# Normed rows as two halves of the positions on 64 partitions each, with the bias of their products added by VectorE

## What is computed

```python
x  = layernorm(h)                                     # 1101 x 64, per batch
sx = einsum('bsh,ndh->bnsd', x, hl_w) + hl_b          # 4 heads of 16
q  = einsum('bnsd,neod->bneso', sx, wq)               # 4 experts a head
k  = einsum('bnsd,nod->bnso', sx, wk);  v = einsum('bnsd,nod->bnso', sx, wv)
att = softmax(einsum('bnesd,bntd->bnest', q, k) * d ** 0.5 + causal)
out = where(sx == 0, 0, einsum('bnest,bntd->bnesd', att, v))
gs  = softmax(out_of_all_experts @ gate_w + gate_b);  mixed = sum_e out_e * gs_e
resid = sx[arange(4), arange(4)]                      # batches 0 to 3, one head each
hn = layernorm(mixed + resid); ... two 16 x 16 layers, norm, a gate over heads
h  = h + result
```

## Time and profile before

| | us |
|---|---|
| runs, median of 3 | 1400.64 (1400.48 to 1404.7) |
| profiled execution | 1396.09, its span 1394.4 |
| TensorE busy | 1100.2 (79%) |
| VectorE busy | 792.6 (57%) |
| ScalarE busy | 755.9 (54%) |
| GpSimd busy | 450.2 (32%) |
| chain that ended last | TensorE 43%, issue 11%, ScalarE 8%, VectorE 6%, GpSimd 3% |

### The profile page before, as it was taken

How to read it: one execution, slowest core, us unless ns; L and a number is a source line. 1 busy time by engine, 2 the same in 40 slices (tenths; PEclk the granted TensorE clock), 3 DMA queues, 4 the chain that set the end, 5 groups by cost and what they waited for, 6 DMA issues and landing times.

```text
span 1394.4 us, 39232 instructions
## 1 busy us (share of the span) xinstructions
PE 1100.2 (79%) x15223; PEld 604.6 (43%) x15223; DVE 792.6 (57%) x1493; ACT 755.9 (54%) x906; POOL 450.2 (32%) x616
## 2 busy tenths in 40 slices
PE   4898538898053799899889889789989988989931
PEld 3455338685031346444345444344434434534410
DVE  4827774316755374476467468458557656752453
ACT  0232124452002575868767767767866876789820
POOL 3000040002411322344343542535434435355431
PEclk9998859995555899999999999989989999999975
DMA  8999059920407427107304603611730730550000
GB/s 152 214 184 214 15 119 197 202 57 1 110 13 134 57 66 115 35 15 141 70 14 109 101 2 89 105 29 41 124 59 15 146 63 15 114 87 3 2 17 10
DMA packets 113981, 113.48 MB, mean 81 GB/s; under 512 B 68072, under 2 KB 85240, under 8 KB 113670
## 3 DMA queue, kind: packets, MB, share of 16 engines
q1 hardware_dynamic: 109776, 110.59, 41.4%
q10 hardware_dynamic: 3733, 0.60, 0.3%
q0 software_dynamic: 320, 0.04, 0.0%
HBM read 88.07 MB, written 22.95 MB: 80 GB/s over the span
## 4 chain that ended last, share of the span: by engine, by line
PE 43%; issue 11%; ACT 8%; DVE 6%; POOL 3%; ACTq 0%; DMA 0%; POOLq 0%; DVEq 0%; SPq 0%
PE b_pso L1983 16%; PE b_pss L1947 14%; ACT b_pb L2062 8%; PE b_psm L2009 4%; PE b_pss L1945 3%; POOL b_pb L2100 2%; PE b_psm L2005 2%; PE b_psm L2026 2%; POOL b_stat L2081 1%; DVE b_rq L2188 1%; PE b_psm L1929 1%; DVE b_ks L2186 1%; PE b_psm L2030 1%; DVE b_squares L2187 1%; PE b_psm L2031 1%
## 5 line engine op out<-in xcount | busy, mean ns | idle before, releaser
L2062 ACT ACTIVATE b_pb<-b_pss 128x1024 f32<-128x1024 f32 (+2 forms) x736 | 649.6, 939 | 308.3 <-PE b_pss L1947 235.4
L1983 PE MATMUL b_pso<-b_pb,b_vop 128*32 128x128 f32 (+4 forms) x4800 | 409.3, 414 | 28.0 <-POOL b_pb L2100 27.9
L2100 POOL TENSOR_SCALAR_AFFINE_SELECT b_pb<-b_pb 128x256 f32<-128x256 f32 (+1 forms) x544 | 259.8, 499 | 504.7 <-ACT b_pb L2062 498.1
L1947 PE MATMUL b_pss<-b_qop,b_kop 97*32 97x512 bf16 (+3 forms) x6144 | 361.0, 337 | 62.1 <-issue 42.4
L1947 PEld LDWEIGHTS b_pss<-b_qop,b_kop 97*32 97x32 bf16 x6144 | 143.2, 97 | 284.4 <-ACT b_pb L2062 153.8
L1983 PEld LDWEIGHTS b_pso<-b_pb,b_vop 128*32 128x32 f32 x4800 | 161.2, 113 | 113.3 <-issue 41.8
L2081 POOL TENSOR_TENSOR b_stat<-b_stat,b_mh 128x18 f32<-128x18 f32 x34 | 110.3, 3263 | 30.2 <-DVE b_stat L2355 18.8
L2276 DVE STREAM_TRANSPOSE b_ot<-b_pso 128x512 f32<-128x512 f32 x64 | 45.9, 717 | 126.6 <-PE b_pso L1983 124.2
L920 PE MATMUL psc<-tz,ub 128*64 128x128 f32 x1152 | 81.0, 286 | 15.7 <-ACT tz L961 8.3
L920 PEld LDWEIGHTS psc<-tz,ub 128*64 128x64 f32 x1152 | 73.1, 143 | 23.5 <-ACT tz L961 11.9
L2009 PE MATMUL b_psm<-b_xt,w_all 65*128 65x384 f32 x144 | 63.4, 562 | 19.0 <-DVE b_rq L2188 16.5
(11 more groups left out here) (394 smaller groups left out, 1315.8 us busy)
## 6 DMA issues: line engine op xcount, KB each, us to landing
b_qop<-qk_parts_b SPq DMA_DIRECT2D x192, 144.0 KB
tz<-taps SPq DMA_DIRECT2D x64, 304.0 KB, 9.5
x<-in_x SPq DMA_DIRECT2D x16, 1024.0 KB, 14.3
qk_parts_b<-b_qs SPq DMA_DIRECT2D x16, 864.0 KB, 5.2
b_kop<-qk_parts_b SPq DMA_DIRECT2D x192, 36.0 KB
qk_parts_b<-b_ks SPq DMA_DIRECT2D x8, 432.0 KB, 3.9
n_late<-id_d SPq DMA_DIRECT2D x1, 2400.0 KB, 9.3
h<-z SPq DMA_DIRECT2D x8, 288.0 KB, 2.8
```

Of the source, the lines that this page charges most:

```text
L1947: mm = pe.matmul(pss[VW * g:VW * g + VW, u % 2, b, col:col + w], lhs, qop[:, n, e, q0:q0 + w], start=True, stop=True, skip_group_check=True)
L1983: mm = pe.matmul(acc, vop[0:P if j < NA - 1 else LAST, j, n, :], rhs, start=(j == 0), stop=(q0 == P * j if x < 2 else j == NA - 1), skip_g ...
L2062: nc.scalar.activation(pb[:, SLOT[un], 0:nb, 0:w], pss[:, s % 2, 0:nb, 0:w], ACT.Exp, scale=float(HD) ** 0.5).then_inc(exped, 1)
L2100: ins = pool.affine_select(out=v_, in_=v_, compare_op=ALU.is_ge, fill=0.0, base=0, pattern=pat, channel_multiplier=-1)
```

## The change

`xt` becomes 128 partitions x 576 positions: the channels of positions 0 to 575 on partitions 0 to 63, those of 576 to 1151 on 64 to 127. The row of ones goes, and with it the bias in the products; `wall` stands twice, on both halves of the partitions, without a bias row. `BLOCKS` lists how the 9 tiles fall on the halves, alternating between them; the middle tile is split in two.

- `turn_rows`: tiles of the lower half of the partitions by transposes, those of the upper by products with the identity, 11 instructions for 9. VectorE takes all out in one copy of 576.
- `tok`, `rmat`: a product per tile on one half or the other, into a bank per half; the middle tile in small pieces. VectorE adds the bias (`vb`, the same on all partitions): three additions for the values' one copy, four for the residual's.
- `feat`: six jobs of two products (lower and upper half, bank 0 and 1) of 288 positions in place of nine products of 384 in five jobs. The bias of a feature is `bcol`, a column; VectorE adds it in the first operation (keys: into `rq`, which gives the banks back at once; queries: into the cast, and again in the difference that gives the banks back).
- `knorm` also waits for `parts`, that is for the second key job as a whole, since the squares are read from `sqk`.
- Slots move: turn 21 to 18, tok 24 to 22, the key jobs 28 and 31 to 26 and 30, the query jobs 37, 41, 45 to 37, 41, 44, 48, qnorm 49 to 52, BOUND 51 to 54, CHECK 25 to 23, fc1, fc2, back 53, 56, 60, 63 to 55, 58, 61, 64.
- In `stage_ssm` two copies make `whad` (head weights twice) and `whab` (head bias on 128 columns), and five more products make `vb` and `bcol`; `vb` and `bcol` are copied out behind the convolution loop, into the place of `wbd`.

```diff
@@ -117,8 +117,11 @@
...
-        self.wbd = sb("w_bd", [NH * HD, WV])
-        self.wall = sb("w_all", [D + 1, WV + NH * VC])
+        over = sb("w_bd", [P, WV])
+        self.wbd = over[0:NH * HD]
+        self.vb = over[:, 0:NH * VC + D]
+        self.bcol = over[:, NH * VC + D:NH * VC + D + 3]
+        self.wall = sb("w_all", [P, WV + NH * VC])
@@ -906,7 +911,12 @@
...
-                pe.matmul(psf[0:D + 1, 1, 0:NH * VC], w.wha[:], w.wvx[:].rearrange("p n c -> p (n c)"), start=True, stop=True).then_inc(wv_done, 1)
+                pe.matmul(psf[:, 1, 0:NH * VC], whad[:], w.wvx[:].rearrange("p n c -> p (n c)"), start=True, stop=True)
+                pe.matmul(psf[:, 1, NH * VC:2 * NH * VC], whab[:], w.wvx[:].rearrange("p n c -> p (n c)"), start=True, stop=True)
+                pe.matmul(psf[:, 1, 2 * NH * VC:2 * NH * VC + D], whab[:], w.wbd[:, WC:WV], start=True, stop=True)
+                for g in range(3):
+                    mm = pe.matmul(psf[:, 1, 2 * NH * VC + D + g:2 * NH * VC + D + g + 1], w.wbd[:, g * P:g * P + P], w.wha[:, D:D + 1], start=True, stop=True)
+                mm.then_inc(wv_done, 1)
@@ -1029,6 +1039,8 @@
...
+                ch.done(cp(whad[:].rearrange("p (u d) -> p u d", u=2), bmid(w.wha[:, 0:D], 2)))
+                ch.done(cp(whab[:], bcast(w.wha[:, D], P)))
@@ -1056,15 +1068,18 @@
...
+                v.wait_ge(wt, 2)
+                ch.done(cp(w.vb, psf[:, 1, NH * VC:2 * NH * VC + D]))
+                ch.step(cp(w.bcol, psf[:, 1, 2 * NH * VC + D:2 * NH * VC + D + 3]))
@@ -1703,6 +1718,10 @@
...
+    HALF, PIECE = LP // 2, LP // 4
+    MIDDLE = NA // 2
+    BLOCKS = [(a + 5 * h, h, P * (a + 5 * h) - HALF * h, P, 0) for a in range(MIDDLE) for h in range(2)]
+    BLOCKS += [(MIDDLE, 0, P * MIDDLE, P // 2, 0), (MIDDLE, 1, 0, P // 2, P // 2)]
@@ -1782,20 +1803,19 @@
...
-        PRO = [(21, "turn", 0), (24, "tok", 0), (28, "feat", ((2, 0), (2, 1))), (31, "feat", ((2, 2),)), (34, "knorm", 0), (37, "feat", ((0, 0), (0, 1)))]
-        PRO += [(41, "feat", ((1, 0), (1, 1))), (45, "feat", ((0, 2), (1, 2))), (49, "qnorm", 0)]
-        EPI = [(53, "fc1", 0), (56, "fc2", 0), (60, "back", 0), (63, "back", 1)]
+        PRO = [(18, "turn", 0), (22, "tok", 0), (26, "feat", (2, 0)), (30, "feat", (2, 1)), (34, "knorm", 0), (37, "feat", (0, 0)), (41, "feat", (0, 1))]
+        PRO += [(44, "feat", (1, 0)), (48, "feat", (1, 1)), (52, "qnorm", 0)]
+        EPI = [(55, "fc1", 0), (58, "fc2", 0), (61, "back", 0), (64, "back", 1)]
...
-        CHECK, BOUND = 25, 51
+        CHECK, BOUND = 23, 54
@@ -1924,9 +1944,14 @@
...
-                    pe.matmul(psm[D:P, 0, 0:P], src[:, NA - 1, :], ident[:], start=True, stop=True)
-                    for a in range(NA - 1):
-                        mm = pe.transpose(psm[0:D, a // 4, a % 4 * P:a % 4 * P + P], src[:, a, :], ident[:])
+                    for a, h, c0, n, off in BLOCKS:
+                        for lo in range(c0 // QT * QT, c0 + n, QT):
+                            x0, x1 = max(c0, lo), min(c0 + n, lo + QT)
+                            out_ = psm[D * h:D * h + D, lo // QT, x0 - lo:x1 - lo]
+                            if n == P and not h:
+                                mm = pe.transpose(out_, src[:, a, :], ident[:])
+                            else:
+                                mm = pe.matmul(out_, src[:, a, :], ident[:, off + x0 - c0:off + x1 - c0], start=True, stop=True)
@@ -1995,29 +2020,37 @@
...
                     if kind == "rmat":
...
-                        for a in range(NA):
-                            mm = pe.matmul(psm[:, 0, a * HD:(a + 1) * HD], xt[:, a * P:(a + 1) * P], wall[:, WC + HD * c:WC + HD * c + HD], start=True, stop=True)
+                        for a, h, c0, n, off in BLOCKS:
+                            r = slice(D * h, D * h + D)
+                            mm = pe.matmul(psm[off:off + n, h, a * HD:(a + 1) * HD], xt[r, c0:c0 + n], wall[r, WC + HD * c:WC + HD * c + HD], start=True, stop=True)
                     elif kind == "tok":
...
-                        for z in range(2):
-                            for a in range(4 * z, 4 * z + 5):
-                                lo, hi = max(NH * VC * a, TOK * z), min(NH * VC * (a + 1), TOK * (z + 1))
-                                mm = pe.matmul(psm[:, z, lo - TOK * z:hi - TOK * z], xt[:, a * P:(a + 1) * P], wall[:, WV + lo - NH * VC * a:WV + hi - NH * VC * a], start=True, stop=True)
+                        for a, h, c0, n, off in BLOCKS:
+                            r = slice(D * h, D * h + D)
+                            if n == P:
+                                o = NH * VC * (a % 5)
+                                mm = pe.matmul(psm[:, h, o:o + NH * VC], xt[r, c0:c0 + n], wall[r, WV:], start=True, stop=True)
+                            else:
+                                for z in range(2):
+                                    mm = pe.matmul(psm[off:off + n, z, 4 * NH * VC:TOK], xt[r, c0:c0 + n], wall[r, WV + NH * VC // 2 * z:WV + NH * VC // 2 * (z + 1)], start=True, stop=True)
                     elif kind == "feat":
...
-                        for i, (g, x) in enumerate(c):
-                            mm = pe.matmul(psm[:, i, 0:FB], wall[:, g * P:g * P + P], xt[:, x * FB:(x + 1) * FB], start=True, stop=True)
+                        g, i = c
+                        for h in range(2):
+                            r = slice(D * h, D * h + D)
+                            mm = pe.matmul(psm[:, h, 0:PIECE], wall[r, g * P:g * P + P], xt[r, PIECE * i:PIECE * i + PIECE], start=True, stop=True)
                     elif kind == "knorm":
+                        pe.wait_ge(parts, (p + 1) * 6 + 2)
@@ -2155,12 +2187,20 @@
...
-                        ch.step(cp(xt[0:D, (NA - 1) * P:], psm[D:P, 0, 0:P]))
-                        give(cp(xt[0:D, 0:(NA - 1) * P], psm[0:D].rearrange("p z q -> p (z q)")))
+                        give(cp(xt[:], psm[:].rearrange("p z q -> p (z q)")[:, 0:HALF]))
                     elif kind == "rmat":
-                        give(cp(resid[:, :, HD * c:HD * c + HD], psm[:, 0, 0:NA * HD].rearrange("p (a d) -> p a d", d=HD)))
+                        for a0, a1, h, lo, hi in ((0, MIDDLE, 0, 0, P), (MIDDLE, MIDDLE + 1, 0, 0, D), (MIDDLE, MIDDLE + 1, 1, D, P), (MIDDLE + 1, NA, 1, 0, P)):
+                            last = tt(resid[lo:hi, a0:a1, HD * c:HD * c + HD], psm[lo:hi, h, a0 * HD:a1 * HD].rearrange("p (a d) -> p a d", d=HD), bmid(vb[lo:hi, NH * VC + HD * c:NH * VC + HD * c + HD], a1 - a0), ALU.add)
+                            if a1 < NA:
+                                ch.step(last)
+                        give(last)
                     elif kind == "tok":
-                        give(cp(vnext[:].rearrange("p a n c -> p (a n c)").rearrange("p (z q) -> p z q", z=2), psm[:, :, 0:TOK]))
+                        w_ = NH * VC
+                        flat = vnext[:].rearrange("p a n c -> p (a n c)")
+                        for h in range(2):
+                            ch.done(tt(flat[:, 5 * w_ * h:5 * w_ * h + 4 * w_].rearrange("p (a q) -> p a q", q=w_), psm[:, h, 0:4 * w_].rearrange("p (a q) -> p a q", q=w_), bmid(vb[:, 0:w_], 4), ALU.add))
+                        ch.wait()
+                        give(tt(flat[:, 4 * w_:5 * w_].rearrange("p (z q) -> p z q", z=2), psm[:, :, 4 * w_:TOK], vb[:, 0:w_].rearrange("p (z q) -> p z q", z=2), ALU.add))
@@ -2169,29 +2209,36 @@
...
                     elif kind == "feat":
-                        i = FEATS.index(c)
...
-                        if g == 2:
-                            dst = lambda t_: ks[:, t_, x * FB:(x + z) * FB].rearrange("p (z q) -> p z q", z=z)
-                        elif x == 0:
-                            dst = lambda t_: qs[:, t_, g, 0:2 * FB].rearrange("p (z q) -> p z q", z=2)
-                        else:
-                            dst = lambda t_: qs[:, t_, :, 2 * FB:]
-                        if i == 0:
+                        g, i = c
+                        at_ = FEATS.index(c)
+                        cut = lambda t_: t_.rearrange("p (z h q) -> p z h q", z=2, h=2)[:, :, i]
+                        dst = (lambda t_: cut(ks[:, t_, :])) if g == 2 else (lambda t_: cut(qs[:, t_, g, :]))
+                        if at_ == 0:
...
-                            ch.done(red(nearest[D:P, x:x + z], psm[D:P, 0:z, 0:min(FB, L - x * FB)], AX.X, ALU.min, apply_absolute_value=True))
-                        ch.step(cp(dst(0), psm[0:m, 0:z, 0:FB]))
-                        ch.step(tt(squares[0:m, slot[c[0]]:slot[c[0]] + z, :], dst(0), dst(0), ALU.mult))
-                        give(tt(rq[0:m, 0:z], psm[0:m, 0:z, 0:FB], dst(0), ALU.subtract))
...
-                        ch.step(cp(dst(1), rq[0:m, 0:z]))
-                        tt(dst(2), rq[0:m, 0:z], dst(1), ALU.subtract).then_inc(parts, 1)
...
+                            rest = rq[0:D]
+                            give(ts(rq[:], psm[:, :, 0:PIECE], bcol[:, 2:3], None, ALU.add))
...
```

(15 more changed lines are left out.)

51 lines of the change are left out of this document (26 added, 25 removed).

## The result

The changed kernel takes 1413.2 us in the median (1410.7 to 1414.5, 4 runs), the kernel before 1400.9 (1400.5 to 1404.7, 4 runs): ratio 1.0080, 95% interval [1.0057, 1.0103]. It is slower by 0.8%, where the forecast was 1374 and faster by 1.9%. The profiled execution went from a span of 1394.4 to 1410.8 us.

What follows compares the result with a forecast made beforehand. TensorE was taken to set the pace in the rewritten part, VectorE close behind. Loop passes -19, first attention pass -7, last passes +0.4, pass without attention -4.6 and convolution +4.0 gave -26 us: 1374, range 1358 to 1401.

Steps and rivals of the forecast that it cites:

- the one on the loop's end: End of a loop pass: moving the bound from slot 51 to 54 was to cost nothing.
- the turn: TensorE's transposes and products of x_n in a loop pass: +0.1 us taken, +0.5 if one behind the other.
- the convolution's delay: Before the convolution loop: VectorE's copies +1.8 us and TensorE's products +2.2, together +4.0, handed on whole.
- Overlap of the halves: Loop pass on TensorE: 64-row products of both halves run together, features -3.0 us, values -1.2.
- The rival without overlap: Halves filling all 128 columns don't overlap: a pass +0.4 to +1.1 us, kernel 1412, slower; chance 0.13.
- Waits: Loop pass, TensorE waiting for VectorE: 1.6 us at the features go, 1.6 come at the key norm.
- VectorE: right: Loop pass: VectorE's keys, queries and copies together were to take 2.1 us more.
- the forecast's 7: First pass with attention: -3.2 us as in a loop pass and four residual products at -0.95 each, -7.
- Net of a pass: Loop pass: terms sum to -4.1 us, a fifth taken off for ScalarE, -3.2 a pass, -19 over six.
- a bound (+9): Convolution stage: +9 us if GpSimd's 10 us operation gets ahead of VectorE's first conv copies.
- a rival with 1379 us: GpSimd's 10 us operation falls ahead of the convolution: 1379 us, inside the forecast's range; no chance given.
- ScalarE as the pace: ScalarE sets the pace, so nothing of TensorE's time reaches the end: 1396 us; chance 0.05.

Runs made afterwards that it cites:

- e2: Changed kernel with 64 already satisfied waits added on TensorE's queue ahead of the passes: 1397.1 us, 1.0046 of before.
- e16: e8 run again unchanged on the chip of e13 to e15: 1364.0 us, 0.9773 of before.
- e9: Kernel before with TensorE's loop over passes 1 to 6 written out: 1358.8 us, 0.9727 of before.
- e14: e8 with the five products and two copies moved behind the convolution loop: 1357.6 us, 0.9713 of before.
- e7: Changed kernel with the edits of e1 and e2 together: 1391.1 us, 0.9905 of before.
- e8: Changed kernel with TensorE's loop over passes 1 to 6 written out, other engines keeping theirs: 1366.8 us, 0.9778 of before.
- e10: e8 with a turn that takes two blocks in one transpose: 1357.9 us, 0.9716 of before.
- e11: e8 plus two-block turn, key norm waiting on the squares, and the convolution's five products and two copies behind its loop: 1333.4 us, 0.9537 of before.
- e13: e8 with the turn back in slot 21, the values in slot 24 and the value check in 25: 1369.4 us, 0.9815 of before.
- e15: e11 with the turn in slot 21 and the values in slot 24: 1327.3 us, 0.9457 of before.
- e5: Changed kernel run once more, unchanged: 1417.8 us, 1.0139 of before.
- e1: Changed kernel with whad and whab copied later and the five products with their copy behind the convolution loop: 1404.7 us, 1.0063 of before.
- e6: Kernel before with 176 already satisfied waits on TensorE's queue ahead of the passes: 1396.5 us, 0.9990 of before.
- e12: Kernel before with 216 already satisfied waits on TensorE's queue ahead of the passes: 1401.8 us, 1.0049 of before.

## Why the prediction was wrong, step by step

The step that failed most is the one on the loop's end: the prediction let nothing there cost time and had no term for the loading of TensorE's code (15 us by e2). Two terms failed in size: the turn, at +0.1 us a pass, measured +1.1, and the convolution's delay, at +4.0 us, measured +14.1 at its first product.

The two kernels with TensorE's loop written out give the layout's account in a pass at full clock. Windows of such a pass, of e16 and of e9:

```profile
594.60:698.10 103.50, 95.55 (x1607) 46.36 (x1603) 72.67 (x141) 80.96 (x95) 46.73 (x74) 1.00 0.41 76
```

```profile
591.40:696.40 105.00, 97.59 (x1589) 48.91 (x1585) 70.53 (x132) 81.35 (x95) 47.60 (x74) 1.00 0.41 74
```

Groups of TensorE in these passes, e16:

```profile
L2045 PE MATMUL b_psm<-b_xt,w_all 64*128 64x288 f32 x24 | 4.5, 455 | 0.0
L1958 PE MATMUL b_psm<-w_ident,b_xn 128*64 128x64 f32 (+1 forms) x14 | 1.9, 262 | 0.0
...
L1956 PE MATMUL b_psm<-w_ident,b_xn 128*64 128x128 f32 x4 | 1.2, 292 | 0.0
L2036 PE MATMUL b_psm<-w_all,b_xt 64*128 64x112 f32 x16 | 1.1, 283 | 0.0
...
L2051 PE MATMUL b_psm<-b_sqk,w_blkkb 64*96 64x384 bf16 x2 | 0.5, 326 | 1.7 <-DVE b_ks L2242 1.7
L2039 PE MATMUL b_psm<-w_all,b_xt 64*64 64x56 f32 x8 | 0.4, 228 | 0.0
```

and e9:

```profile
L2013 PE MATMUL b_psm<-b_xt,w_all 65*128 65x384 f32 x18 | 7.1, 515 | 1.1 <-DVE b_rq L2192 1.1
L2009 PE MATMUL b_psm<-w_all,b_xt 65*128 65x112 f32 (+1 forms) x20 | 2.5, 279 | 0.0
...
L1933 PE MATMUL b_psm<-w_ident,b_xn 128*64 128x128 f32 x8 | 1.1, 276 | 0.0
...
L2018 PE MATMUL b_psm<-b_squares,w_blkkb 64*96 64x384 bf16 x2 | 0.5, 326 | 0.5 <-DVE b_rq L2192 0.5
L1931 PE MATMUL b_psm<-w_ident,b_xn 128*64 128x128 f32 x2 | 0.4, 298 | 0.0
```

The turn of these two passes by the windows of `b_xn`, again e16 and e9:

```profile
594.60:698.10 103.50, 2.54 (x18) 1.00 0.41 76
```

```profile
591.40:696.40 105.00, 1.43 (x10) 1.00 0.41 74
```

- **Overlap of the halves: right.** Features 7.1 to 4.5 us, -2.6 (forecast -3.0; a job is 0.76 us, not 0.69), values 2.5 to 1.5, -1.0 (-1.2). The rival without overlap, 1412 us, came near the measured time by a mechanism that isn't there.
- **Waits: right.** 1.6 to 1.7 us (forecast: 1.6 go, 1.6 come). **VectorE: right**, +2.1 us a pass (70.53 to 72.67).
- **The turn, "I take +0.1": mis-sized, +1.1.** 1.4 us became 2.5, beyond the +0.5 of my upper bound. The timelines show why, first before and then changed:

```profile
593.26 0.43 PE L1927 MATMUL b_psm<-w_ident,b_xn 128*64 128x128 f32 x2
593.63 1.06 PE L1929 MATMUL b_psm<-w_ident,b_xn 128*64 128x128 f32 x8
```

```profile
715.37 0.30 PE L1952 MATMUL b_psm<-w_ident,b_xn 128*64 128x128 f32 x1
715.60 0.43 PE L1954 MATMUL b_psm<-w_ident,b_xn 128*64 128x128 f32 x2
715.96 0.30 PE L1952 MATMUL b_psm<-w_ident,b_xn 128*64 128x128 f32 x1
716.19 0.43 PE L1954 MATMUL b_psm<-w_ident,b_xn 128*64 128x128 f32 x2
```

  A transpose and a product for the other column half start 0.23 us apart, and the next transpose 0.36 us later, 0.59 a pair. Before, a product takes 0.37 us to the next start and eight transposes in a row 1.06, 0.13 each: 0.50 for one of each, one behind the other. So the pair, which shares all 128 rows, does not run side by side. I had carried over the overlap of row halves to column halves, for which no row of mine stood, and even my bound without it was too low. It also holds for the four turns of pass 0's residual, which I had left out of that pass's sum: 10.25 us of TensorE (windows of the tile `b_h`) where before has 6.02, while the residual products gave 3.5 (8.7 to 5.2). These 4.2 us and the turn's own 1.1 or more (that pass was not all at full clock) are as much as pass 0, with 1.9 us won, is short of the forecast's 7, though no run separates them. Pass -1, whose turn at 1.2 GHz goes from 2.5 to 4.1, won 3.5 up to the first score and not 4.6. The first score itself came 11.0 us later (453.3), not 0.6 earlier.
- **Net of a pass.** In the two passes above -1.5 us (forecast -3.2); but the three intervals of e9 wholly at full clock take 105.0 to 105.1 us and those of e16 and e14 103.6, 105.1 and 103.4, so it is -1.0 in the mean. In the kernels that keep the loop and have no second stall at the 14th record it is about as much: 557.3 and 557.4 us over five passes in e2 and e7, before 564.4, -1.4 a pass. Written out, nothing is left over all five passes (105.8 in e9, 106.0 in e8, 105.3 in e16): TensorE was at 1.2 GHz for 31 us in e8 and 17 in e16, and 7 in e9. The other written-out profiles of the new layout have 31 (e10), 17 (e11, e13), 27 (e14) and 10 us (e15), all more than the single one of e9. The reason is not shown; e13 speaks against the turn's slot.
- **"The bound's move costs nothing", and nothing else at the loop's end: the step that failed most.** The prediction had no term for code. The changed kernel stands a second time 14 records behind its loop's top, as it would if a 16 KB block of its code ended there: 10.4 us in itself, 15 us by e2. The five intervals were forecast to gain 16 us and lost 8; of these 24 us e2 gives back 15, and the turn's 1.1 or more a pass makes up most of the rest. The trace of before showed the 4.5 us of "issue" at the loop's top, which I had read as given.
- **The convolution stage, "+4.0": right for VectorE's delay, wrong for what follows from it.** VectorE came 4.5 us later, and so just past the start of GpSimd's 10 us operation; the first product came 14.1 us later instead of 4.0. I had this as a bound (+9) and as a rival with 1379 us "inside the range", without comparing the two starts: 196.3 + 4.0 = 200.3 against 200.5 in the trace, a margin of 0.2 us. In other profiles (e2 to e5, e16) one copy slipped in ahead, the first product came at 201.9 to 203.2 and the loop still ended at 304. e1 and e14 took away the delay and the hold together, and the loop's end was back at 292 to 293. The Trainium skill, Advanced Engine Details and Errata, section VectorE Performance Modes, says that a VectorE instruction that uses two ports and a GpSimd instruction block each other. The traces agree, for whab (8.48 us beside GpSimd's copy, where whad takes 0.18 just ahead of it) and for tz.
- **ScalarE as the pace:** it fell as the only bound. ScalarE still waits for TensorE's scores for 21.7 us in e16's pass and 23.1 in e9's, and e10, whose edit shortens TensorE's turn and lengthens VectorE's work, gained 1.3 us a pass.
- **Small slips in the working.** Two key jobs of 4.65 us with 0.2 and 0.15 make 9.65 and not 9.8. The turn's five products are those of the upper half of the partitions, not the lower, and two of them have 64 columns, as have the two of the middle tile.

With both the code's place and the hold mended the changed kernel was at 0.9905 [0.9867, 0.9942] of before (e7), half of the gain forecast, and in the profiled execution part of that was luck, the short stretch behind the convolution. The turn was a third error of its own.

## What to carry to other kernels

A long loop on TensorE can cost a stall each time it returns to its top, and how long depends on where the code lies. Read the "issue" gaps there before and after an edit, and try writing out that engine's loop: it won 3.6% for the changed kernel (0.9778 for 1.0139 of before, e8 and e5) and 2.7% for the one before (e9). Two edits that differ in instruction count differ in the code's place too: compare them with the loop written out. When an edit delays an engine, list what other engines start in the next microseconds at fixed times, and compare the starts, not the lengths.

## What the runs showed of the hardware

- A return to the loop's top on TensorE cost 2.8 to 5.3 us in loops of some 1600 records a pass. In the written-out kernels (e8 to e11, e13 to e16) there was no such gap at these places, and at most one of 1.1 to 1.6 us elsewhere in the passes. The Trainium skill, Runtime: NRT & Kernel Launch, section Instruction fetch mechanics, has code fetched in 16 KB blocks and a stall where a branch leaves the window; the trace agrees (128 packets, 2.10 MB), and adds a second stall of 0.8 to 3.5 us, 14 or 45 records behind the target, which comes and goes with the place of the code (e2, e6, e12).
- Row halves of TensorE overlap with full 128 columns and 288 moving columns (0.76 us a pair, where two of 288 columns one behind the other take 1.23); a transpose and a product on column halves don't (0.59 us a pair, 0.50 one behind the other).
- A VectorE copy that starts 0.08 us behind the start of GpSimd's 9.9 us operation waits for it (11.76 us for three copies that take 2.09); one that starts 0.06 us ahead of it does not, and the two behind it do (e16).
- The moment at which the clock falls in the same stream of products (to the 1.2 GHz level, 4, 20 or 42 us behind the loop's end) moved the stretch behind the convolution between 81.4 and 104.7 us from profile to profile, in kernels whose 463 records there are the same (e1, e7, e14, e15). No run here explains it.
